# Placing each query tile's causal mask matmuls directly behind its scores

## The chip, the cores and the metric

The kernel runs on one core of a Trainium2 chip. The metric is the device time of one launch in microseconds (us). Lower is better. The engines are called by their names in the profile: PE is the tensor engine's matmul stream and PEld its weight loads, DVE the vector engine, ACT the scalar engine, POOL the GpSimd engine, SP the engine that issues most of the DMAs.

## The reference

The reference is a two-layer decoder block over 8 batches of 256 tokens of 512 features: cross-attention to an image context, a quantised feed-forward layer, a second cross-attention, and a last block with latent causal self-attention and a mixture of experts. Only the causal self-attention of that last block is touched. Cut to what matters, for each batch and each of 16 heads (`HD` = 32):

```python
scores = jnp.einsum('bqhd,bkhd->bhqk', q, k) * scale
causal = jnp.tril(jnp.ones((s, s), dtype=bool))
scores = jnp.where(causal[None, None], scores, jnp.finfo(scores.dtype).min)
probs = jax.nn.softmax(scores, axis=-1)
out = jnp.einsum('bhqk,bkhd->bqhd', probs, v).reshape(b, s, H)
```

## The kernel before, in words

The program is written as five stages, one behind the other, each with its own instruction stream per engine. Nothing schedules them: the order on an engine is the order in which the Python code issues the instructions, and semaphores join the engines. The stage in question is `latent_attention`. It works through the 8 batches in nine turns of `for i in TURNS` (i = -1 to 7). In turn i, PE finishes the attention of batch i and prepares batch i+1, and the two are woven together.

The 16 heads of a batch are taken in four calls (c = 0 to 3) of four heads (j = 0 to 3). A head has 32 features, so its query and key lie on 32 partitions, and the four heads of a call lie on the four partition groups of 32. `scores(s, c)` computes the scores of batch s for the sole purpose of finding each query's peak. For each of the two query tiles (t = 0 and 1, of 128 queries) it issues three products of split operands (`qt_hi` by `kt_lo`, `qt_hi` by `kt_hi`, `qt_lo` by `kt_hi`), each for four heads. Each of these matmuls uses 32 rows of the array, and the four heads of a product use four different row groups. This text calls four such matmuls a tiled group. Query tile t writes columns t·128 to t·128+255 of four banks of `s_ps`, one bank for each head.

The causal mask is added on PE too: a full-array matmul of the bf16 identity `ident_b` with the bf16 matrix `mask` (-1e30 above the diagonal) accumulates onto the 128x128 diagonal block of a head. There are eight of these in a call: four heads for each of two query tiles. The last of them raises `s_ready`. `find_peak` on DVE waits for it, reduces the two query tiles with two instructions (L2714 and L2715) and raises `peak_done`, and only then may the next call of `scores` start, for it overwrites `s_ps`.

There are 32 calls of `scores` in the stage: four in turn -1 for batch 0, and four in each of the turns 0 to 6. In those turns PE has other work between the calls: `inverses` and `outputs` (the projection with `first_out` and `wq`), `values`, and from the next turn on `latents` and `turn_peaks`. `turned_scores` (L2408 and L2411) computes the scores a second time, transposed, with the same kind of tiled groups, and `weigh` and `masses` (L2425 and L2436) use tiles of 32 columns. In the trace, `L47`, `L48` and `L49` are the three products of the helper `split_product`, all with full-array matmuls, and L2318 is a full-array transpose.

Of the kernel before, what the change touches and what calls it, by code (L numbers as in the profile page):

```python
# [25 lines left out]
TB = SEQ // P  # L26
# [2064 lines left out]
def latent_attention(nc, x_res, h_res, h_sq, ident, begun, handed, picks, w_dram, rope_dram, late, expert_dram, expert_rows):  # L2091
# [24 lines left out]
    with ExitStack() as ctx:  # L2116
# [82 lines left out]
        def await_free(eng, name, s):  # L2199
            eng.wait_ge(free_of(name, s), use_of[name, s] // BANKS + 1)  # L2200
# [106 lines left out]
        def _(pe):  # L2307
# [66 lines left out]
            def scores(s, c):  # L2374

                if c == 0:
                    if s > 0:
                        pe.wait_ge(exp_done, 2 * C * s)
                    for name in ("kt0", "kt1", "qt0", "qt1"):
                        await_free(pe, name, s)  # L2380
                else:
                    pe.wait_ge(peak_done, C * s + c)
                for t in range(TB):
                    tok = slice(t * P, (t + 1) * P)
                    cols = slice(t * P, t * P + SEQ)
                    for n, (q, k) in enumerate(((qt_hi, kt_lo), (qt_hi, kt_hi), (qt_lo, kt_hi))):
                        for j in range(4):
                            mine = slice(HD * j, HD * (j + 1))
                            pe.matmul(s_ps[:, j, cols], q[mine, c, tok], k[mine, c, :], start=n == 0, stop=n == 2)
                for t in range(TB):  # L2390
                    for j in range(4):
                        mm = pe.matmul(s_ps[:, j, 2 * t * P:(2 * t + 1) * P], ident_b[:, :], mask[:, :], start=False, stop=True,
                                       skip_group_check=True)
                mm.then_inc(s_ready, 1)
# [64 lines left out]
            for i in TURNS:  # L2459
# [41 lines left out]
                if nxt:  # L2501
                    if i == -1:
                        pe.wait_ge(mask_done, 1)
                    scores(i + 1, 0)
# [9 lines left out]
                if nxt:  # L2514
                    scores(i + 1, 1)
                if now:
                    outputs(i, 1, 0)
                if nxt:
                    values(i + 1, 1)
                    scores(i + 1, 2)  # L2520
# [1054 lines left out]
```

## Time and profile before

| What | us |
|---|---|
| Median of 3 runs | 2353.2 |
| Lowest and highest run | 2352.92, 2355.69 |
| The profiled execution | 2352.92 |
| Its span in the trace | 2351.2 |
| PE busy in the span | 2200.7 (94%) |
| DVE, ACT, POOL busy | 1317.1, 999.1, 798.4 |

The busy shares are means over all stages. The calls of `scores` start between 1717.8 and 1995.4 us of the span; what they are worth has to be read from that stretch. In a row of the timeline, several instructions of one line that follow each other are merged; the row gives the start of the first, the time to the end of the last, and the count. A matmul's duration contains its way through the array, so consecutive matmuls overlap, and the distance between their starts is what each costs PE.

### The profile page before, as it was taken

Reading aid. Unit: us, or ns where it says so; the run is one execution under the profiler, and the core shown is the slowest. Engines: PE = TensorE matmul, PEld = TensorE weight load, DVE = VectorE, ACT = ScalarE, POOL = GpSimd, SP = SyncE. Lnnn points to the kernel's source line nnn. Section 1 sums busy time; section 2 is a strip of 40 time slices with the busy share of each in tenths; the row PEclk is TensorE's granted clock in tenths of the full one; section 3 lists DMA queues with packets and bytes.
Section 4 is the critical chain, followed back from the end, with each engine's and each line's share of the span. In section 5 each row is a group of like instructions: output and inputs, shape, how many; then the busy total and the mean of one; then the engine's idle time right before and its main releaser. Section 6 shows DMA issues by size and latency. Waiting matters only on the chain. (4 is left out here: it accounts for less than half of the span.)

```text
span 2351.2 us, 42185 instructions
## 1 busy us (share of the span) xinstructions
PE 2200.7 (94%) x17406; PEld 1806.1 (77%) x17406; DVE 1317.1 (56%) x2355; ACT 999.1 (42%) x1770; POOL 798.4 (34%) x687
## 2 busy tenths in 40 slices
PE   6999998689979999999999999999889999899996
PEld 4666676344458888898999998988768787799996
DVE  6666775588874344433443335444554545677764
ACT  4777433377843223222332223222255554425553
POOL 3111110366522222222323222333154553224664
PEclk9999998799989999999999999999999999899998
DMA  6454202100021002111111012110000000247996
GB/s 251 159 170 131 73 2 109 54 1 1 1 81 66 34 28 81 72 37 37 46 54 69 31 36 97 37 46 19 1 25 2 2 2 28 82 152 238 274 274 120
DMA packets 45342, 177.49 MB, mean 75 GB/s; under 512 B 5984, under 2 KB 5984, under 8 KB 38880
## 3 DMA queue, kind: packets, MB, share of 16 engines
q1 hardware_dynamic: 35296, 151.72, 18.2%
q0 software_dynamic: 9856, 23.07, 4.8%
q8 instruction: 139, 2.28, 0.4%
q14 instruction: 51, 0.42, 0.1%
HBM read 143.84 MB, written 30.93 MB: 74 GB/s over the span
## 5 line engine op out<-in xcount | busy, mean ns | idle before, releaser
L247 POOL TENSOR_TENSOR c_prob<-c_prob,c_inv_mass 128x512 f32<-128x512 f32 x128 | 130.4, 1040 | 438.0 <-DVE c_inv_mass L239 438.0
L229 ACT ACTIVATE c_prob<-c_s_ps,c_neg_peak 128x256 f32<-128x256 f32 x256 | 117.8, 473 | 360.6 <-DVE c_neg_peak L218 360.6
L47 PE MATMUL c_ring<-bc_xt_lo,bc_wq_hi 128*128 128x256 f32 x512 | 152.1, 297 | 5.4 <-POOL bc_xt_lo L1675 5.4
L47 PE MATMUL c_ring<-c_ctx_lo,c_w_hi 128*128 128x256 f32 x512 | 146.5, 286 | 0.0
L48 PE MATMUL c_ring<-bc_xt_hi,bc_wq_hi 128*128 128x256 f32 x512 | 146.2, 286 | 0.0
L49 PE MATMUL c_ring<-bc_xt_hi,bc_wq_lo 128*128 128x256 f32 x512 | 146.1, 285 | 0.0
L49 PE MATMUL c_ring<-c_ctx_hi,c_w_lo 128*128 128x256 f32 x512 | 143.4, 280 | 0.0
L48 PE MATMUL c_ring<-c_ctx_hi,c_w_hi 128*128 128x256 f32 x512 | 143.2, 280 | 0.0
L1679 POOL TENSOR_TENSOR c_ctx_lo<-c_ctx_f,c_ctx_hi 128x1024 fp32r<-128x1024 f32 x32 | 78.2, 2444 | 166.9 <-ACT c_ctx_hi L1868 166.9
L203 PE MATMUL c_s_ps<-c_kt,c_qt 128*128 128x256 f32 x512 | 121.7, 381 | 3.0 <-ACT c_prob L229 3.0
L1201 POOL TENSOR_TENSOR b_hw<-b_h,b_lnw 128x512 f32<-128x512 f32 x64 | 96.2, 1519 | 78.8 <-DVE b_h L1375 78.8
L1675 POOL TENSOR_TENSOR bc_xt_lo<-c_xt_f,bc_xt_hi 128x1024 fp32r<-128x1024 f32 x32 | 79.1, 2471 | 127.4 <-ACT bc_xt_hi L1862 127.4
L286 PE MATMUL c_o_ps<-c_prob_t,c_v 128*128 128x256 f32 x512 | 117.6, 384 | 0.9 <-ACT c_prob_t L276 0.9
L2052 DVE SCALAR_TENSOR_TENSOR x_res<-c_ring,c_gain,x_res 128x512 f32<-128x512 f32 x64 | 47.8, 750 | 114.0 <-PE c_ring L49 114.0
L295 DVE TENSOR_TENSOR c_o_lo<-c_o_ps,c_o_hi 128x1024 fp32r<-128x1024 f32 x32 | 39.2, 1224 | 127.6 <-ACT c_o_hi L291 127.6
L47 PE MATMUL c_ring<-c_w_lo,c_ctx_hi 128*128 128x512 f32 x256 | 110.2, 430 | 0.0
L286 PEld LDWEIGHTS c_o_ps<-c_prob_t,c_v 128*128 128x128 f32 x512 | 98.2, 193 | 15.3 <-issue 1.3
L1944 DVE COPY c_kt<-c_ring 128x512 f32<-128x512 f32 x64 | 44.2, 691 | 116.7 <-PE c_ring L49 116.7
L1944 DVE COPY c_qt<-c_ring 128x512 f32<-128x512 f32 x64 | 44.3, 691 | 116.2 <-PE c_ring L49 116.2
L203 PEld LDWEIGHTS c_s_ps<-c_kt,c_qt 128*128 128x128 f32 x512 | 94.9, 190 | 16.4 <-ACT c_prob L229 3.8
L3023 POOL DMA_INDIRECT out<-el_r,e_target x44 | 81.4, 1849 | 72.7 <-DMA out<-el_r,e_target 57.9
L47 PEld LDWEIGHTS c_ring<-bc_xt_lo,bc_wq_hi 128*128 128x128 f32 x512 | 99.5, 194 | 6.6 <-POOL bc_xt_lo L1675 5.8
(540 smaller groups left out, 6980.5 us busy)
## 6 DMA issues: line engine op xcount, KB each, us to landing
x_res<-b_w SPq DMA_DIRECT2D x48, 512.0 KB, 4.7
e_raw<-e_w SPq DMA_DIRECT2D x15, 1536.0 KB, 8.7
bc_raw<-c_w SPq DMA_DIRECT2D x16, 1024.0 KB, 5.9
c_ctx_f<-ctx_t SPq DMA_DIRECT2D x32, 512.0 KB, 3.5
c_xt_f<-xnt_scratch SPq DMA_DIRECT2D x24, 512.0 KB, 3.2
h_res<-e_w SPq DMA_DIRECT2D x7, 1536.0 KB, 10.1
wq_scratch<-x_res SPq DMA_DIRECT2D x24, 256.0 KB, 2.5
ab_wq<-wq_scratch SPq DMA_DIRECT2D x3, 2048.0 KB, 13.1
```

The lines of the kernel that those rows point to most:

```text
L47: pe.matmul(out, lhs[0], rhs[1], start=first, stop=False)
L48: pe.matmul(out, lhs[0], rhs[0], start=False, stop=False)
L49: return pe.matmul(out, lhs[1], rhs[0], start=False, stop=last)
L203: mm = pe.matmul(self.s_ps[:, j, 0:w], q_of(u, j), k_of(u, j)[:, 0:w], start=mask is None, stop=True, skip_group_check=mask is not None)
L229: ins = act.activation(self.prob[:, u % 2, j, 0:w], self.s_ps[:, j, 0:w], ACT.Exp, bias=self.neg_peak[:, u % 2, j:j + 1], scale=self.scale ...
L247: pool.tensor_tensor(part, part, self.inv_mass[:, u % 2, js].unsqueeze(2).to_broadcast([P, 2, w]), ALU.mult).then_inc(self.prob_done, 1)
L286: mm = pe.matmul(out_of(g, j), v_of(g, j, t), self.prob_t[:, buf, t, j, :], start=(t == 0), stop=(t == TB - 1))
L1201: pool.tensor_tensor(hw[:, n % 2, cols], h[:, n % 2, cols], lnw[:, cols], ALU.mult).then_inc(hw_done, 1)
L1675: pool.tensor_tensor(xt_lo[:, :, :], xt_f[:, :, :], f32(xt_hi[:, :, :]), ALU.subtract).then_inc(xt_lo_done, 1)
L1679: pool.tensor_tensor(ctx_lo[:, :, :], ctx_f[:, :, :], f32(ctx_hi[:, :, :]), ALU.subtract).then_inc(ctx_lo_done, 1)
L1944: dve.tensor_copy(to, bank_of(f"f{k}", s)).then_inc(free_of(f"f{k}", s), 1)
L3023: pool.indirect_dma_start(out=out[:, :], out_offset=bass.IndirectOffsetOnAxis(ap=target[:, TB * j + t:TB * j + t + 1], axis=0), in_=r[:, j ...
```

## The change

One line is removed: the second `for t in range(TB):` loop. The four mask matmuls of a query tile now stand inside the first loop, behind the three tiled groups of the same query tile. Before, they stood in a loop of their own behind both query tiles. The matmuls, their operands, flags and counts are the same, and so is the semaphore, which the last mask matmul of the call raises.

```diff
--- before.py
+++ after.py
@@ -2387,7 +2387,6 @@
                         for j in range(4):
                             mine = slice(HD * j, HD * (j + 1))
                             pe.matmul(s_ps[:, j, cols], q[mine, c, tok], k[mine, c, :], start=n == 0, stop=n == 2)
-                for t in range(TB):
                     for j in range(4):
                         mm = pe.matmul(s_ps[:, j, 2 * t * P:(2 * t + 1) * P], ident_b[:, :], mask[:, :], start=False, stop=True,
                                        skip_group_check=True)
```

On PE, the end of call c = 0 of batch 0 changes as follows (the first turn; `d_kt`, `d_qt` are keys and queries, L2318 turns the inputs of batch 1):

```order
 L2389 MATMUL d_s_ps<-d_kt_hi,d_qt_hi 128x256 x4
 L2389 MATMUL d_s_ps<-d_kt_hi,d_qt_lo 128x256 x4
+L2391 MATMUL d_s_ps<-d_mask,d_ident_b 128x128 x4
 L2389 MATMUL d_s_ps<-d_kt_lo,d_qt_hi 128x256 x4
 L2389 MATMUL d_s_ps<-d_kt_hi,d_qt_hi 128x256 x4
 L2389 MATMUL d_s_ps<-d_kt_hi,d_qt_lo 128x256 x4
-L2392 MATMUL d_s_ps<-d_mask,d_ident_b 128x128 x8
+L2391 MATMUL d_s_ps<-d_mask,d_ident_b 128x128 x4
 L2318 MATMUL d_ring<-ident,d_a 128x128 x8
```

Four of the eight mask matmuls moved up: they now stand behind the third tiled group, and four stay behind the sixth. The line number drops by one, since the file is a line shorter.

On PE in a later turn, where `outputs` (here with `d_first_out`) follows a call of `scores`:

```order
 L2389 MATMUL d_s_ps<-d_kt_hi,d_qt_hi 128x256 x4
 L2389 MATMUL d_s_ps<-d_kt_hi,d_qt_lo 128x256 x4
+L2391 MATMUL d_s_ps<-d_mask,d_ident_b 128x128 x4
 L2389 MATMUL d_s_ps<-d_kt_lo,d_qt_hi 128x256 x4
 L2389 MATMUL d_s_ps<-d_kt_hi,d_qt_hi 128x256 x4
 L2389 MATMUL d_s_ps<-d_kt_hi,d_qt_lo 128x256 x4
-L2392 MATMUL d_s_ps<-d_mask,d_ident_b 128x128 x8
+L2391 MATMUL d_s_ps<-d_mask,d_ident_b 128x128 x4
 L47 MATMUL d_ring<-d_first_out_lo,d_o_hi 128x512
 L48 MATMUL d_ring<-d_first_out_hi,d_o_hi 128x512
```

The same four moved, and what follows the call is the same full-array product. No other engine's order changes.

## Rows read from the trace of the kernel before

**Rows 1.** Part 1 of the page: busy time, share of the span, instructions.

```profile
PE 2200.7 (94%) x17406; PEld 1806.1 (77%) x17406; DVE 1317.1 (56%) x2355; ACT 999.1 (42%) x1770; POOL 798.4 (34%) x687
```

**Rows 2.** Busy time in stretches: turns 0 to 6, and one turn of them.

```profile
core 0: us, PE busy (x) PEld busy (x) DVE busy (x) ACT busy (x) POOL busy (x), PEclk, DMA share, GB/s
1741.00:1983.00 242.00, 239.78 (x3348) 190.68 (x3346) 126.16 (x165) 128.89 (x221) 129.27 (x186) 1.00 0.02 5
1870.81:1908.09 37.28, 37.03 (x509) 29.53 (x508) 19.26 (x25) 19.87 (x35) 19.26 (x27) 1.00 0.01 2
```

**Rows 3.** All waits of PE between 1741 and 1983: total, times, longest.

```profile
PE d_ring L2318 <- DVE d_qt_lo L2707: 1.7, 7, 0.3
PE d_s_ps L2389 <- DVE d_kt_lo L2707: 0.5, 1, 0.5
```

**Rows 4.** Timeline of PE, a call of `scores`: start, us, instruction, count, idle before.

```profile
1874.26 0.40 PE L49 MATMUL d_ring<-d_first_out_hi,d_o_lo 128*128 128x512 f32 x1
1874.59 0.39 PE L2389 MATMUL d_s_ps<-d_kt_lo,d_qt_hi 32*128 32x256 f32 x4
1874.81 0.29 PE L2389 MATMUL d_s_ps<-d_kt_hi,d_qt_hi 32*128 32x256 f32 x4
1874.93 0.28 PE L2389 MATMUL d_s_ps<-d_kt_hi,d_qt_lo 32*128 32x256 f32 x4
1875.05 0.29 PE L2389 MATMUL d_s_ps<-d_kt_lo,d_qt_hi 32*128 32x256 f32 x4
1875.17 0.29 PE L2389 MATMUL d_s_ps<-d_kt_hi,d_qt_hi 32*128 32x256 f32 x4
1875.29 0.28 PE L2389 MATMUL d_s_ps<-d_kt_hi,d_qt_lo 32*128 32x256 f32 x4
1875.51 0.62 PE L2392 MATMUL d_s_ps<-d_mask,d_ident_b 128*128 128x128 bf16 x8
1875.94 0.47 PE L47 MATMUL d_ring<-d_first_out_lo,d_o_hi 128*128 128x512 f32 x1
```

**Rows 5.** Line 2392 of PE: count, shortest, median and longest duration in ns.

```profile
L2392 PE MATMUL d_s_ps<-d_mask,d_ident_b x256: 218/220/267, 1718.7 to 1995.4; 128*128 128x128 bf16 x128
```

**Rows 6.** Timeline of PE, full-array matmuls of 256 columns before a tiled group.

```profile
1891.29 0.28 PE L48 MATMUL d_ring<-bc_wq_hi,bc_xt_hi 128*128 128x256 f32 x1
1891.41 0.28 PE L49 MATMUL d_ring<-bc_wq_hi,bc_xt_lo 128*128 128x256 f32 x1
1891.62 0.39 PE L2408 MATMUL d_s_ps<-d_qt_hi,d_kt_lo 32*128 32x256 f32 x4
```

**Rows 7.** Timeline of PE, the last call for batch 0 and what follows.

```profile
1729.05 0.67 PE L2392 MATMUL d_s_ps<-d_mask,d_ident_b 128*128 128x128 bf16 x8
1733.36 0.58 PE L47 MATMUL d_ring<-bc_xt_lo,bc_latent 128*128 128x256 f32 x1 [3.64 <-POOL bc_xt_lo L2233]
```

**Rows 8.** Timeline of ACT in the first turn.

```profile
1719.80 1.09 ACT L2545 ACTIVATE d_at_f<-d_ring 128x512 f32<-128x512 f32 x2 [2.94 <-PE d_ring L2318]
1720.97 1.06 ACT L2551 ACTIVATE bc_xt_hi<-d_at_f 128x1024 fp32r<-128x1024 f32 x1
1721.93 2.91 ACT L2538 ACTIVATE h_res<-x_res,bc_shift,bc_row_rstd 128x512 f32<-128x512 f32 x4
1724.75 0.57 ACT L2577 ACTIVATE d_v<-d_ring 128x512 f32<-128x512 f32 x1
1725.23 1.04 ACT L2531 ACTIVATE d_first_out_hi<-d_raw 128x1024 fp32r<-128x1024 f32 x1
```

**Rows 9.** Timeline, behind the last call for batch 7.

```profile
1994.97 0.62 PE L2392 MATMUL d_s_ps<-d_mask,d_ident_b 128*128 128x128 bf16 x8
1995.63 0.69 DVE L2714 TENSOR_REDUCE d_neg_peak<-d_s_ps 128x4 f32<-128x512 f32 x1 [0.78 <-PE d_s_ps L2392]
1997.51 0.44 PE L2371 MATMUL d_ring<-ident,d_neg_peak 128*128 128x128 f32 x2 [1.92 <-DVE d_neg_peak L2715]
```

**Rows 10.** Busy time in stretches around the end of the first turn.

```profile
1721.00:1729.50 8.50, 5.18 (x99) 4.13 (x99) 3.83 (x5) 6.22 (x8) 3.15 (x2) 1.00 0.01 3
1729.50:1736.30 6.80, 3.16 (x17) 2.94 (x14) 1.82 (x2) 0.00 (x0) 3.81 (x2) 0.50 0.00 0
```

## The prediction, made before the changed kernel ran

> **What bounds the kernel now.** I read the page's busy times first, then the stretches, then PE's waits, then the timeline of one call. PE is busy 94% of the span [rows 1], but that is a mean over five stages. In the 242 us between 1741 and 1983, which hold the calls of `scores` of turns 0 to 6, PE is busy 239.78 us at a granted clock of 1.00, while DVE, ACT and POOL are busy about half of the time [rows 2]. PE's waits of that stretch sum to 2.2 us: seven short ones for the split of the turned queries and one for that of the turned keys [rows 3]. None of them stands behind a wait for a peak: the four calls of a turn are far enough apart that DVE's reduction is done. So in turns 0 to 6, what PE spends more or less goes straight into the time. A turn takes 37.28 us with 37.03 us of PE [rows 2]. The chain of waits begins only after this stage, so it says nothing of it; the stretches do.
>
> **What the call costs.** The timeline of one undisturbed call shows four distances [rows 4]. Tiled groups follow each other at 0.12 us (1874.93, 1875.05, 1875.17, 1875.29). The first mask matmul starts 0.22 us after the sixth group: 0.10 us late. The eight masks end 0.62 us after the first began and one lasts 0.22 us [rows 5], so they follow each other at (0.62 - 0.22) / 7 = 0.057 us. At the call's begin, the step from full-array to tiled work shows two losses. The first tiled group starts only when the full-array matmul before it has 0.07 us left of its duration: 1874.26 + 0.40 - 0.07 = 1874.59 [rows 4]. The same is seen behind a shorter one: 1891.41 + 0.28 - 0.07 = 1891.62, where without a switch the distance was 0.12 us [rows 6]. And the first tiled group lasts 0.39 us instead of 0.28 and the second starts 0.22 us after it instead of 0.12: its weights are not loaded ahead.
>
> **The change, term by term.** It removes nothing and adds no instruction. It moves four mask matmuls per call from the end to the middle, and there PE has to switch from tiled to full-array and back once more.
>
> - Into the masks, behind the third group: 0.22 instead of 0.12 us, +0.10.
> - The four masks themselves: 4 x 0.057 us in the middle, 4 x 0.057 us fewer at the end, 0.
> - Back to the tiled groups, behind the fourth mask: this step without a wait isn't in the trace of before. By the rule of the two rows above, the group starts 0.07 us before the mask's end: 0.22 - 0.07 = 0.15 us after its start instead of 0.057, +0.09. From below it is bounded by the masks' own distance (+0.00), from above by the longest distance seen into a tiled group, 0.33 us behind a 512-column matmul [rows 4], +0.27. I take 0.09, since the 256- and the 512-column row obey one rule although they differ in distance.
> - The first tiled group of the second query tile loads its weights uncovered: 0.22 instead of 0.12 us between starts, 0.39 instead of 0.28 in duration, +0.11. Bounded below by 0 (weights hidden under the masks).
> - The end of the call, from the last tiled group to mask and from mask to the next work, is as it was: 0.
>
> The sum is 0.10 + 0.09 + 0.11 = 0.30 us per call, with bounds of 0.10 and 0.48.
>
> **How many calls are on the path.** There are 32. The 28 of turns 0 to 6 are, by the above, since PE doesn't idle there. The last call for batch 7 is among them: DVE waits for its masks (0.78 us), PE waits for DVE (1.92 us), and a later mask shifts the rest [rows 9]. Of the four calls of the first turn, three are hidden: behind the last one PE idles 3.64 us until POOL has split the inputs of batch 1 [rows 7], and three later calls take 3 x 0.30 = 0.9 us of this. If that cover were gone they would cost these 0.9 us. The first of the four is not hidden: behind it stand the transposes of batch 1's inputs, for which ACT waits (2.94 us), and from then on ACT works without a gap through 1726.3 [rows 8] toward the very split that PE waits for. So 28 + 1 = 29 calls count: 29 x 0.30 = 8.7 us.
>
> On the other engines nothing moves. What hangs on `s_ready` is `find_peak`, now 0.30 us later behind each call; in turns 0 to 6 the next call comes later by the same, so no new wait forms.
>
> The profiled execution took 2352.92 us, 1.7 us more than its span and 0.3 us less than the median. Its sum is 2352.92 + 8.7 = 2361.6; from the median it is 2353.2 + 8.7 = 2361.9 us, +0.37%.
>
> **A rule weighed.** In the rows, the successor of another shape starts 0.07 us before the recorded end of the matmul before it, at each of the three switches [rows 4, 6]. The Trainium skill, TensorEngine Tiling (Array Packing), Key Properties, says that a change of the tiling mode drains the engine. Taken word for word, with nothing begun before the end, each of the two added switches would cost 0.07 us more, 0.44 us per call in all. The trace agrees with the rule in kind and shows the drain overlapped by these 0.07 us.
>
> The other rule speaks for a smaller price. Within tiled work the trace shows weights loaded ahead, since the groups stand 0.12 us apart; at a switch it does not, by the 0.39 us group [rows 4]. The Trainium skill, TensorE: Matmul & The Clock Gate, The mechanism, says that a weight load is pulled ahead of matmuls in flight when its row group doesn't conflict or the background buffer takes it. The masks fill all row groups, so the background buffer would have to take it; what that gives is the second rival.
>
> **The rivals.**
>
> 1. *Full drain.* Each added switch waits for the complete end of the matmuls before it: (0.30 + 2 x 0.07) x 29 = 12.8 us, 2366.0 us. For it: only that the step from a mask to a tiled group hasn't been seen undisturbed. Against it: the 0.07 us hold for both directions.
> 2. *Weights hidden, only the entry counts.* The second tile's weights are loaded under the masks, and the step out of the masks costs no more than their own distance: 0.10 x 29 = 2.9 us, 2356.1 us, within 0.2%. For it: there are four masks of 0.057 us, time enough for a load. Against it: in rows 4 and 6 the load ahead would have had a longer matmul to hide under, and didn't.
> 3. *The delay doesn't reach the end.* Another engine's chain sets the pace of a turn, and PE's 0.30 us fall into its idle time: about 2353.2 us. Against it: 0.25 us of idle PE in a turn of 37.28 [rows 2] can't take in 4 x 0.30 us, and even these waits follow PE's own transposes.
> 4. *The other side: the masks ride in the shadow of the tiled groups.* A tiled group lasts 0.28 us but costs 0.12; the remaining 0.16 us are its way through the array. If masks that stand between two query tiles could run in that shadow, four of them, 4 x 0.057 = 0.23 us, would vanish from each call: 29 x 0.23 = 6.7 us less, 2346.5 us. It decides from an added price below zero, so only if the mask follows a group at 0.12 us or sooner. Against it: the same step at the call's end takes 0.22 us [rows 4].
>
> The clock moves the sum a little: after the first turn's calls it falls to 0.50 from 1729.5 to 1736.3, where PE had waited for DVE and then for POOL [rows 7, 10]. PE's idle time there shrinks from 3.64 to 2.7 us. If the clock stayed up, the work from 1733.36 to 1736.3 would take half: at most 1.5 us back. This stays inside the range of the forecast.
>
> **How the numbers follow.** A change of 0.2%, 4.7 us, is about what a measurement of this kernel can tell from none. The forecast has 0.80, the full drain 0.07, hidden weights 0.06, a delay that doesn't arrive 0.04, the shadow 0.03. The forecast's own range comes from the roundings of the rows, 0.27 to 0.34 us per call, from 29 to 32 calls, from the clock, and from a median that may stand an us off: 0.27 x 29 - 1.5 - 1 = 5.3 up to 0.34 x 32 + 1 = 11.9 us, 2358.5 to 2365.1. I let the range reach to the full drain at the upper end, 2366.2, and leave out the others, 0.13 in sum. Slower has 0.80 + 0.07 = 0.87; within 0.2% 0.06 + 0.04 = 0.10; faster 0.03.
>
> **What would show it.** In the changed kernel's timeline, a call should read: third tiled group, +0.22 us the first mask, four masks at 0.057, +0.15 us behind the fourth a tiled group of 0.39 us, +0.22 us the next. A turn should take 37.28 + 4 x 0.30 = 38.5 us with PE's idle time unchanged, and the wait for POOL behind the first turn should be shorter by 0.9 us. A turn of 37.7 us would speak for hidden weights, one of 39.0 for a full drain, one of 37.3 for a delay absorbed elsewhere. The prediction is wrong if masks follow a tiled group at 0.12 us, or if PE's idle time in turns 0 to 6 falls.

## The result, and the profile after

| | before | after |
|---|---|---|
| Median of 6 runs, us | 2354.44 | 2369.61 |
| Lowest and highest, us | 2351.43, 2358.65 | 2364.32, 2374.07 |
| Span of the trace, us | 2351.2 | 2364.0 |

The ratio of after to before is 1.0057 (95% interval 1.0043 to 1.0073), 13.4 us slower. It rests on 19 executions of the changed kernel, whose median is 2367.82 us; the table has the first six of them. Measured twice more against new runs of before, the ratio was 1.0055 (1.0037 to 1.0073) and 1.0042 (1.0028 to 1.0056). The direction was forecast; the time lies above the range of 2358.5 to 2366.2, and even the range's upper end is 3.4 us short of it.

The page of after, part 1, answers to [rows 1]. The instructions are the same, and PE is busy 14.6 us longer, more than the time between the spans.

```profile
PE 2215.3 (94%) x17406; PEld 1809.9 (77%) x17406; DVE 1316.0 (56%) x2355; ACT 1000.6 (42%) x1770; POOL 794.9 (34%) x687
```

The timeline of PE in after, a call at the same place of a turn (turn 0), answers to [rows 4]:

```profile
1767.62 0.40 PE L49 MATMUL d_ring<-d_first_out_hi,d_o_lo 128*128 128x512 f32 x1
1767.94 0.39 PE L2389 MATMUL d_s_ps<-d_kt_lo,d_qt_hi 32*128 32x256 f32 x4
1768.17 0.29 PE L2389 MATMUL d_s_ps<-d_kt_hi,d_qt_hi 32*128 32x256 f32 x4
1768.29 0.28 PE L2389 MATMUL d_s_ps<-d_kt_hi,d_qt_lo 32*128 32x256 f32 x4
1768.50 0.40 PE L2391 MATMUL d_s_ps<-d_mask,d_ident_b 128*128 128x128 bf16 x4
1768.83 0.39 PE L2389 MATMUL d_s_ps<-d_kt_lo,d_qt_hi 32*128 32x256 f32 x4
1769.05 0.28 PE L2389 MATMUL d_s_ps<-d_kt_hi,d_qt_hi 32*128 32x256 f32 x4
1769.17 0.28 PE L2389 MATMUL d_s_ps<-d_kt_hi,d_qt_lo 32*128 32x256 f32 x4
1769.39 0.40 PE L2391 MATMUL d_s_ps<-d_mask,d_ident_b 128*128 128x128 bf16 x4
1769.59 0.47 PE L47 MATMUL d_ring<-d_first_out_lo,d_o_hi 128*128 128x512 f32 x1
```

Every step is as forecast. The first mask starts 0.21 us after the third group. The fourth mask starts 0.18 us after the first (0.40 - 0.22), and the next tiled group 0.15 us after that: 1768.83. That group lasts 0.39 us, and its successor starts 0.22 us later. From the first tiled group to the first product behind the call, after takes 1.65 us; before took 1.35 us [rows 4].

The stretch of turns 0 to 6 and one turn of it in after, against [rows 2]; then the waits of PE from 1741 to 1995, against [rows 3]:

```profile
1741.00:1983.00 242.00, 240.50 (x3187) 187.92 (x3190) 122.93 (x163) 123.91 (x213) 122.88 (x175) 1.00 0.01 2
1763.89:1802.44 38.55, 38.30 (x513) 29.76 (x512) 17.91 (x23) 19.94 (x35) 19.28 (x27) 1.00 0.01 2
```

```profile
PE d_ring L2318 <- DVE d_qt_lo L2706: 1.8, 7, 0.3
PE d_s_ps L2389 <- DVE d_kt_lo L2706: 0.5, 1, 0.5
```

A turn takes 38.55 us instead of 37.28, and PE is idle for the same 0.25 us in it. No wait is new.

What was not forecast is the first turn. Here are three stretches of before, each cut at the start of the first tiled group of a call: the first turn (first call for batch 0 to first call for batch 1), the 24 calls for batches 1 to 6, and from the last call of all to the first matmul of the expert stage. The columns are those of [rows 2]; the third from the right is the granted clock.

```profile
1717.79:1758.95 41.16, 33.15 (x488) 26.66 (x488) 24.52 (x40) 21.40 (x35) 22.58 (x28) 0.92 0.01 2
1758.95:1982.18 223.23, 221.27 (x3041) 176.37 (x3041) 112.40 (x141) 117.49 (x202) 115.21 (x162) 1.00 0.01 4
1994.05:2027.30 33.25, 22.75 (x324) 16.40 (x323) 17.63 (x27) 14.01 (x23) 9.52 (x11) 0.88 0.01 1
```

And the same of after, with two parts of its first turn behind them:

```profile
1720.48:1763.85 43.37, 37.83 (x488) 29.82 (x488) 24.32 (x40) 21.55 (x35) 22.59 (x28) 0.84 0.01 2
1763.85:1994.68 230.83, 228.79 (x3041) 177.78 (x3041) 112.47 (x141) 117.76 (x202) 115.25 (x162) 1.00 0.01 4
2007.30:2042.48 35.18, 24.59 (x323) 17.92 (x323) 17.63 (x27) 14.03 (x23) 9.63 (x11) 0.85 0.00 1
...
1721.90:1725.30 3.40, 3.19 (x28) 2.63 (x24) 1.82 (x2) 1.53 (x3) 0.00 (x0) 0.50 0.00 0
1732.10:1742.30 10.20, 7.96 (x55) 7.05 (x56) 2.42 (x4) 0.39 (x1) 5.22 (x3) 0.50 0.01 2
```

The 24 calls grew by 7.60 us, 0.32 each, at a clock of 1.00. The first turn grew by 2.21 us, not by 0.3: the clock fell to 0.50 (1.2 GHz) twice, for 3.4 and for 10.2 us, where it had fallen once in before, for 6.8 us [rows 10]. The last stretch grew by 1.93 us, 1.6 us more than its one call explains.

The same stretches in all traces (us; the last column is from the first matmul of `latent_attention` to the last of the expert stage):

| Kernel | First turn | 24 calls | Last call to expert stage | Both stages |
|---|---|---|---|---|
| before | 41.16 | 223.23 | 33.25 | 629.2 |
| before, again | 41.14 | 223.17 | 33.23 | 629.2 |
| after | 43.37 | 230.83 | 35.18 | 639.9 |
| after, second | 43.36 | 230.81 | 35.09 | 639.8 |
| after, third | 43.38 | 230.74 | 33.70 | 639.5 |
| first batch only | 43.33 | 223.30 | 33.38 | 628.2 |
| later batches only | 41.28 | 230.79 | 34.84 | 637.4 |
| one mask in the middle | 43.49 | 230.83 | 33.67 | 639.6 |
| after, filled | 41.63 | 230.74 | 34.58 | 638.6 |
| first call only | 43.36 | 223.25 | 34.74 | 632.2 |
| first call delayed | 42.87 | 223.24 | 34.51 | 630.4 |
| same delay, no switch | 43.22 | 230.66 | 36.01 | 640.5 |
| no masks | 41.06 | 214.39 | 32.68 | 617.1 |
| no masks, filled | 40.95 | 214.27 | 32.68 | 617.9 |

One stretch isn't in the table, from the stage's first matmul to the first call of `scores`. It takes 12.80 to 12.83 us in twelve of the fourteen traces. In two variants, the first batch alone and the same delay in all calls, it takes 11.28 and 11.45 us, and the clock doesn't fall in it, although nothing ahead of the first call differs. Here it is for before, the first batch alone and the same delay:

```profile
1704.97:1717.79 12.82, 9.57 (x55) 8.30 (x56) 6.25 (x15) 6.34 (x11) 4.96 (x9) 0.87 0.34 106
...
1707.55:1718.83 11.28, 8.26 (x55) 6.93 (x56) 7.06 (x15) 6.34 (x11) 5.24 (x9) 1.00 0.39 121
...
1708.10:1719.55 11.45, 8.25 (x55) 6.95 (x56) 7.22 (x15) 6.34 (x11) 5.25 (x9) 1.00 0.38 119
```

So in these two the falls of the clock lay differently from the start, and their first turns can't be set beside the others alone.

### The profile page after: what moved, and what is told of

Read it like the earlier page. It is cut to its first block and busy times, and to the rows that moved or that the text cites. A ratio compares the mean times of both kernels' runs of the same rounds, so it can differ in the third digit from the quotient of the medians.

```text
span 2364.0 us, 42185 instructions
## 1 busy us (share of the span) xinstructions
PE 2215.3 (94%) x17406; PEld 1809.9 (77%) x17406; DVE 1316.0 (56%) x2355; ACT 1000.6 (42%) x1770; POOL 794.9 (34%) x687
```

## The experiments

All of them change `scores` alone, except the filled ones and the three that repeat a kernel. The ratio is always to the kernel before, run on the same chip. The diffs are against the kernel before and are cut: `pe.matmul(...)` stands for the mask matmul as it was. Two variants, the first call alone and the first call delayed, were executed once each, so only their traces are read.

**The changed kernel again.** 

> The changed kernel once more, to see what repeats. In its first trace each call of scores in turns 0 to 6 costs 0.31 us more, 28 of them 8.7 us, as forecast. But the first turn cost 2.2 us where 0.3 was forecast (clock at 0.50 for 13.7 us instead of 6.8), and 2.7 us were lost before the stage began. Theory A (clock): the extra switches make PE's clock fall for longer in the first turn, in every execution; then the first turn again costs 1.5 to 2.5 us more than 0.3, and the time is 11 to 13 us over before. Theory B (chance): the extra is where clock dips happen to fall; then the first turn costs 0.3 to 1 us in this trace, and the time over many runs is 9 us over before.

Measured: ratio 1.0055 (1.0037 to 1.0073); first turn 43.36 us at clock 0.84, as in the first trace. The first turn's extra repeats, and so does its absence in the second trace of before (41.14 us): it belongs to the kernel. A part of the first trace's difference was chance all the same: the stage begins at 1705.0 us in the trace of before and at 1707.7 and 1710.4 in these two, with no instruction changed ahead of it.

**The first batch alone.** 

> Only the four calls of scores for batch 0 (the first turn) have their masks placed per query tile; the 28 others are as before. Theory A (the first turn's clock falls longer because of the switches): 2 to 3 us slower than before, with more than 6.8 us at clock 0.50 between the first call and turn 0. Theory B (chance): 0.3 us slower, no difference that can be measured, and the calls of turns 0 to 6 cost what they did.

```diff
-                for t in range(TB):
-                    for j in range(4):
+                    for tt, j in ([(t, j) for j in range(4)] if s == 0 else []):
                         mm = pe.matmul(...)
+                for tt, j in ([] if s == 0 else [(t, j) for t in range(TB) for j in range(4)]):
+                    mm = pe.matmul(...)
```

Measured: ratio 1.0001 (0.9990 to 1.0012). The trace has the longer first turn, with the clock mean that after has in it:

```profile
1718.83:1762.16 43.33, 37.41 (x489) 29.39 (x490) 24.53 (x40) 21.52 (x35) 22.58 (x28) 0.84 0.01 2
```

Both stages together are 1.0 us shorter than before. The first turn is 2.2 us longer, but the stretch ahead of the first call is 1.5 us shorter (11.28 instead of 12.82), and the expert stage ran 1.8 us faster. From the stage's first matmul to the first call for batch 1 the extra is thus only 0.6 us (54.61 against 53.98), so this trace doesn't show what the four calls cost. The time doesn't either: its interval goes from -2.4 to +2.8 us. The trace of the first call alone, below, has the usual 12.80 us ahead of it and decides.

**The later batches alone.** 

> The four calls of the first turn are as before, the 28 of turns 0 to 6 have their masks placed per query tile. Theory A: 28 x 0.31 = 8.7 us slower, the first turn as in the kernel before. Theory B: also 8.7 us, so this one and the changed kernel differ by 0.3 us. A third reading, that the extra comes behind the stage (the last turn and the start of the expert stage at another phase), gives 11 us or more here.

The edit is the same with the two conditions exchanged. Measured: ratio 1.0035 (1.0022 to 1.0048), 8.2 us with an interval of 5 to 11 us. The trace:

```profile
1720.55:1761.83 41.28, 33.21 (x489) 26.77 (x490) 24.52 (x40) 21.42 (x35) 22.60 (x28) 0.92 0.01 2
1761.83:1992.62 230.79, 228.76 (x3042) 177.81 (x3041) 112.47 (x141) 117.60 (x202) 115.28 (x162) 1.00 0.02 4
```

The first turn is as before, and the 24 calls have grown by 7.56 us. Both stages together are 8.2 us longer, near the forecast's 8.7. The interval can't tell this from the 10.7 us of the changed kernel's trace; the 41.28 us of the first turn in the trace can.

**One mask in the middle, seven at the end.** 

> One mask matmul instead of four stands between the two query tiles of every call; the other seven stand at the end. If the price is that of the two switches of shape (0.10 in, 0.09 out, 0.11 for the first tiled group) and not of the masks, a call of turns 0 to 6 again costs 0.31 us more, and a turn 38.5 us. If each mask in the middle has a price of its own, a quarter of it stays: 0.08 us a call, a turn of 37.6 us.

```diff
-                for t in range(TB):
-                    for j in range(4):
+                    for tt, j in ([(0, 0)] if t == 0 else []):
                         mm = pe.matmul(...)
+                for tt, j in [(t, j) for t in range(TB) for j in range(4)][1:]:
+                    mm = pe.matmul(...)
```

Measured: ratio 1.0051 (1.0036 to 1.0067), the 24 calls 230.83 us. The middle of a call in its trace:

```profile
1769.99 0.28 PE L2389 MATMUL d_s_ps<-d_kt_hi,d_qt_lo 32*128 32x256 f32 x4
1770.21 0.23 PE L2391 MATMUL d_s_ps<-d_mask,d_ident_b 128*128 128x128 bf16 x1
1770.37 0.39 PE L2389 MATMUL d_s_ps<-d_kt_lo,d_qt_hi 32*128 32x256 f32 x4
1770.59 0.29 PE L2389 MATMUL d_s_ps<-d_kt_hi,d_qt_hi 32*128 32x256 f32 x4
```

One mask costs the call as much as four did: 0.22 us in, 0.16 us out (0.23 - 0.07), and again a group of 0.39 us. The price is that of the two switches, and a mask in the middle adds none of its own.

**The kernel before as a control.** 

> The kernel before itself, as a control: what its trace shows when taken again. In the first trace of it, the stage of scores begins at 1705.0 us of the span; in the traces of five variants it begins 2.6 to 5.4 us later, although no instruction ahead of it differs. If that is chance, this trace begins later too (1707 to 1710), and the ratio to the kernel before is 1.000 within 0.15%. The first turn, from the first call of scores to the first call of turn 0, should again take 41.2 us if its length belongs to the kernel; if it varies by chance, up to 43.4 us as in the four variants with switches in the first turn.

Measured: ratio 0.9991 (0.9980 to 1.0003). The stage begins at 1707.0, 2.1 us later than in the first trace, and then repeats it to 0.06 us in every stretch up to the expert stage. So what lies ahead of the stage differs from run to run, and the stage's own length didn't in these two.

**PE kept at work in the first turn.** 

> The changed kernel with 118 added mask-sized bf16 matmuls (0.057 us each) into the unused output bank where PE waits in the first turn (15, 18, 30 and 55 of them, 0.9 to 3.1 us, shorter than the waits of 1.0, 1.2, 1.9 and 3.6 us). Theory A (PE's idle stretches and switches in the first turn let the clock fall, which costs 1.9 us over the forecast): with PE kept at work the clock stays up, the first turn shrinks from 43.4 to about 40 us, and the time falls by 3 us against the changed kernel, to a ratio of about 1.004. Theory B (the clock falls by chance, or the idle time is not what matters): first turn 43 us, ratio 1.0055.

```diff
+            def filler(count):
+                for _ in range(count):
+                    pe.matmul(o_ps[:, 0, 0:P], ident_b[:, :], mask[:, :], start=True, stop=True)
```

Measured: ratio 1.0034 (1.0024 to 1.0044); the first turn takes 41.63 us. The calls of `filler` are added where the expectation says, in the first turn alone. The clock of that turn, first the low stretch and then the rest:

```profile
1722.00:1725.40 3.40, 3.40 (x29) 3.34 (x27) 1.82 (x2) 1.67 (x3) 0.00 (x0) 0.50 0.00 0
1725.40:1762.10 36.70, 36.06 (x555) 29.35 (x553) 21.55 (x36) 19.82 (x33) 22.62 (x28) 1.00 0.01 2
```

The short fall of 3.4 us stays, the long one of 10.2 us is gone, and the turn is 1.74 us shorter although PE has 118 matmuls more to do. It is gained behind the wait for POOL: PE takes that work up 17.37 us after the first call's start (16.89 in after: the last fill runs on past the end of POOL's split, which comes at 1737.3 in this trace), and from there to the first call for batch 1 it needs 24.26 us instead of 26.48. So the low clock is what most of the first turn's extra was lost to. The forecast of 40 us had both falls gone.

**The first call alone.** 

> Only the very first call of scores (batch 0, c = 0) has its masks placed per query tile. In the four variants whose first turn has the switches, a clock dip begins 1 to 2 us behind the first call's start, and the later one lasts 10.2 instead of 6.8 us. If the first call's switches bring the first of these dips, the trace shows it here, and the first turn takes 42 us or more. If it needs the switches of all four calls, the trace reads as before: one dip of 6.8 us, 41.5 us (0.3 more for this call).

The edit is that of the first batch alone, with the condition `s == 0 and c == 0`.

Measured: the first turn takes 43.36 us at clock 0.84, behind the usual 12.80 us. The two falls of 3.4 and 10.2 us are those of after. The switches of one call, 0.3 us, bring the whole 2.2.

**The first call delayed, without a switch.** 

> The order of before; behind the first call's masks (batch 0, c = 0) six mask matmuls once more, 0.34 us, no switch. With the switches in this one call the first turn took 43.37 us. If the switches did it, 41.5 us here; if a third of a microsecond's delay is enough, 43.4 us.

```diff
-                for t in range(TB):
-                    for j in range(4):
+                for tt, j in [(t, j) for t in range(TB) for j in range(4)] + (
+                        [(1, j) for j in range(4)] + [(1, 3)] * 2 if s == 0 and c == 0 else []):
                         mm = pe.matmul(...)
```

Measured: 42.87 us, 1.71 more than before for an added 0.34. Here are the first turn, the low stretch in it, and PE's first work behind the wait:

```profile
1721.36:1764.23 42.87, 35.16 (x494) 28.64 (x494) 24.52 (x40) 21.52 (x35) 22.32 (x28) 0.88 0.01 2
...
1733.10:1743.30 10.20, 6.87 (x35) 6.61 (x34) 2.33 (x4) 0.84 (x3) 4.12 (x2) 0.50 0.00 0
```

```profile
1737.28 0.58 PE L47 MATMUL d_ring<-bc_xt_lo,bc_latent 128*128 128x256 f32 x1 [3.33 <-POOL bc_xt_lo L2233]
```

In before, PE came back from the wait at 1733.36 [rows 7] and had worked 2.9 us when the clock rose at 1736.3. Here it came back at 1737.28, 4.2 us into the low stretch instead of 3.9, and the clock rose only at 1743.3, after 6 us of work at half speed. No switch was added, so the long stretch needs none: in this trace a third of a microsecond's delay was enough. It is different with the short fall of 3.4 us. It isn't here, while each of the seven traces with switches in the first call has a fall that begins 0.9 to 1.8 us after that call's start. Of the seven traces without them only the next variant's has one there. That the switches bring this fall is likely from this, but not shown.

**The same delay in all calls, without a switch.** 

> The order of before, and at the end of each of the 32 calls of scores five or six mask matmuls once more (5.5 x 0.057 = 0.31 us, added to elements that are masked already). So each call is as much longer as in the changed kernel, but with full-array work instead of two switches of shape. Turns 0 to 6 should again grow by 28 x 0.31 = 8.7 us under every theory. If the switches make the clock fall in the first turn, the first turn here has one dip of 6.8 us and takes 41.5 us, as before plus 0.3. If it is the delay or its phase that does it, 43.4 us. The last turn (30.0 us before, 31.6 to 31.9 in kernels that arrive there 8 to 11 us later) takes 31.6 or more if that is a matter of when it starts, 30.3 if it is the switches. In time: ratio 1.0037 or so in the first case, 1.0050 in the second.

```diff
-                for t in range(TB):
-                    for j in range(4):
+                for tt, j in [(t, j) for t in range(TB) for j in range(4)] + (
+                        [(1, j) for j in range(4)] + [(1, 3)] * (1 + (c % 2 == 0))):
                         mm = pe.matmul(...)
```

Measured: ratio 1.0041 (1.0026 to 1.0057); first turn 43.22 us, the 24 calls 230.66 us. Its first turn and its last stretch:

```profile
1719.55:1762.77 43.22, 36.11 (x511) 29.55 (x511) 24.36 (x40) 21.52 (x35) 22.58 (x28) 0.92 0.01 2
...
2006.06:2042.07 36.01, 25.60 (x328) 18.86 (x328) 17.62 (x27) 14.02 (x23) 9.62 (x11) 0.81 0.01 2
```

Calls that are as long as in the changed kernel, with full-array work in place of the switches, give a kernel as slow as it, within the intervals. For the 24 calls this is what PE's work adds up to. The first turn agrees in length, but not in the way to it. Its mean clock is 0.92, with two falls of 3.4 us, and the first of them begins 0.6 us after the first call's start, ahead of the first added matmul. Here are the last three tiled groups of that call, which stand ahead of all its masks; the third takes 0.48 us where it took 0.31 in before:

```profile
1719.98 0.31 PE L2389 MATMUL d_s_ps<-d_kt_lo,d_qt_hi 32*128 32x256 f32 x4
1720.10 0.40 PE L2389 MATMUL d_s_ps<-d_kt_hi,d_qt_hi 32*128 32x256 f32 x4
1720.23 0.48 PE L2389 MATMUL d_s_ps<-d_kt_hi,d_qt_lo 32*128 32x256 f32 x4
```

So the delay can't have brought that fall. With the shorter stretch ahead of the first call, this run takes 54.67 us from the stage's first matmul to the first call for batch 1, against 53.98 in before and 56.19 in after. It doesn't show that a delay costs the first turn what the switches do.

**No mask matmuls.** 

> The eight mask matmuls of each call of scores are left out, so the peaks are found over all keys and not over the causal ones; a softmax doesn't depend on which peak is subtracted, and the causal cut of the probabilities by POOL stays. In the trace of before, the sixth tiled group to the second full-array product behind the masks takes 0.21 + 0.43 + 0.31 = 0.95 us; without masks it is 0.21 + 0.34 = 0.55 as behind L2411. So 0.40 us less per call, 29 calls on the path: 11.6 us faster than before, ratio 0.995. If a switch between two shapes cost nothing by itself, the gain would be the masks alone, 8 x 0.057 = 0.45 us a call and 13.1 us; if the calls weren't on the path, nothing.

```diff
-                            pe.matmul(s_ps[:, j, cols], q[mine, c, tok], k[mine, c, :], start=n == 0, stop=n == 2)
-                for t in range(TB):
-                    for j in range(4):
-                        mm = pe.matmul(...)
+                            mm = pe.matmul(s_ps[:, j, cols], q[mine, c, tok], k[mine, c, :], start=n == 0, stop=n == 2)
```

Measured: ratio 0.9952 (0.9937 to 0.9966), 11.3 us faster than before. The 24 calls take 214.39 us, 0.37 less each. A call of it in the timeline, from the sixth group on:

```profile
1765.32 0.29 PE L2389 MATMUL d_s_ps<-d_kt_hi,d_qt_lo 32*128 32x256 f32 x4
1765.54 0.50 PE L47 MATMUL d_ring<-d_first_out_lo,d_o_hi 128*128 128x512 f32 x1
1765.88 0.39 PE L48 MATMUL d_ring<-d_first_out_hi,d_o_hi 128*128 128x512 f32 x1
```

From the sixth group to the first product are 0.22 us; before they were 0.65 [rows 4]. Of these 0.43, 0.03 are lost to the product itself, which stands directly behind tiled work and takes 0.50 instead of 0.47. The switch stays, for full-array work must follow, and only the masks' own time goes. This version beats both kernels. Its first turn, 41.06 us, has a low stretch of 10.2 us too, from 8.6 us after the first call's start, with no delay added anywhere. It ends as early as in before (18.8 instead of 18.5 us), so its length alone doesn't make a turn longer. What counts is how much of PE's work behind the wait for POOL falls into it: 2.9 us in before, 3.7 here, 4.9 in after and 6.0 with the first call delayed.

**No masks, filled.** 

> The kernel without mask matmuls (the peaks over all keys), with the same 118 added matmuls where PE waits in the first turn. In the changed kernel they took the first turn from 43.4 to 41.6 us. Without masks the first turn takes 41.1 us with a clock dip of 10.2 us; PE waits there 0.9, 1.0, 1.9 and 4.8 us. If the fill keeps the clock up as there, the first turn takes 39 to 39.5 us and the time falls by a further 1.7 us, to a ratio of 0.9945 to before; if the fill only moves the waits, 0.9952 as without it.

Measured: ratio 0.9961 (0.9947 to 0.9974), no gain over the version without fill. The last fill ends at 1734.7, PE's wait for POOL only at 1737.04, and from there the clock is low for 3.4 us:

```profile
1732.00:1737.00 5.00, 2.75 (x50) 2.57 (x47) 1.44 (x2) 0.00 (x0) 4.99 (x3) 1.00 0.00 0
1737.00:1740.40 3.40, 3.36 (x15) 3.36 (x16) 0.00 (x0) 0.38 (x1) 0.00 (x0) 0.50 0.00 0
```

The expected gain of 1.7 us didn't come.

**A third measurement of the change.** 

> The changed kernel a third time, to see whether its timed excess is larger than what its traces add up. From the stage's begin to the last matmul of the expert stage, its two traces are 10.7 us longer than the two of before (639.8 and 639.9 against 629.1 and 629.2), a ratio of 1.0045; the two timed ratios were 1.0057 and 1.0055. If the trace has everything, the third ratio lies near 1.0045, the stretch again takes 639.8 us and the first turn 43.4 us. If the switches cost more in executions that aren't profiled, it lies at 1.0055 or above again.

Measured: ratio 1.0042 (1.0028 to 1.0056), first turn 43.38 us, both stages 639.5 us. The ratio lies near what the trace adds up to (10.3 us, 1.0044).

## Why the prediction was right or wrong

*PE bounds the stage:* right for turns 0 to 6. The 24 calls' 7.60 us arrived in full, and PE's idle time in a turn stayed at 0.25 us. *The delay doesn't reach the end* is out.

*The price of a call, 0.30 us:* right, and term by term. Measured 0.32 over the 24 calls; the rows of after show 0.21 us in, 0.15 out and the group of 0.39 us. The one unseen term, the step from a short mask back to a tiled group, was taken from the rule of two other rows (0.07 us before the end) and came out at 0.15 as worked out. In one of those two rows, at the begin of a call, PE's code also waits for `peak_done` at the same place, so the late load of the weights might have been that wait's. In the middle of a call no wait stands in the code, and the group takes 0.39 us there too: it is the change of shape. *Full drain* asked for 0.22 us there and *hidden weights* for a group of 0.28: both are out. The full drain's 2366.0 us came nearer to the measured time than the forecast did, for a reason that has nothing to do with it. *The masks in the shadow* is out by the 0.21 us. The experiment with one mask shows that the switches make the price.

*Three of the first turn's calls are hidden, and the fourth costs 0.30 us:* this step failed. The first turn cost 2.2 us. The order of the waits is as the prediction has it: PE still waits there for POOL's split. But that wait is 1.6 us shorter in the trace of after (2.01 instead of 3.64), not 0.9:

```profile
1737.37 0.58 PE L47 MATMUL d_ring<-bc_xt_lo,bc_latent 128*128 128x256 f32 x1 [2.01 <-POOL bc_xt_lo L2233]
```

What the prediction took for granted is that the clock's low stretch stays where it was or shrinks: "at most 1.5 us back", and nothing for a longer one. The runs showed a cost of 1.9 us in its place, at two points. First, a fall of 3.4 us came at the end of the first call, on the very path that the prediction calls not hidden. These are the transposes of batch 1's inputs, before and after:

```profile
1719.16 1.04 PE L2318 MATMUL d_ring<-ident,d_a 128*128 128x128 f32 x8
...
1722.33 1.91 PE L2318 MATMUL d_ring<-ident,d_a 128*128 128x128 f32 x8
```

They take 0.87 us longer, ACT and POOL follow them, and PE comes back from its wait 16.89 us after the first call's start instead of 15.57: 1.32 us later, where 0.30 was forecast. Second, the long low stretch lasted 10.2 us instead of 6.8, so 4.9 us of PE's work behind the wait ran at 1.2 GHz instead of 2.9 us: another 0.89 us. The two make the 2.21 us. With PE kept at work 1.74 us came back. A delay of 0.3 us in the first call alone, with switches or without, brought 2.2 and 1.7 us, in one trace each.

*The last call for batch 7 costs one more 0.30:* the stretch from it to the expert stage grew by 1.93, 1.85 and 0.45 us in the three traces of after. The expert stage behind it took 306.9 us in both traces of before and 305.1, 305.1 and 306.2 in those of after. The two changes sum to +0.1, +0.1 and -0.2 us, so the forecast's 0.30 for this call isn't seen in the sum, and no other cost is either. The clock's falls lie differently around the border of the two stages in before and after; that this hides the 0.30 isn't shown.

The sum of the trace is then 2.21 (first turn) + 7.60 (24 calls) + 0.75 (the next three) + 1.93 (last call and last turn) - 1.79 (expert stage) = 10.7 us, where 8.7 were forecast. That is a ratio of 1.0045. It lies within all three intervals. The mean of the three ratios, 1.0051, is 1.4 us above it; whether this difference is real isn't shown.

*The base and the range:* this failed too, beside the mechanism. The median of three runs, 2353.2, was below those that came later (2354.4, and 2354.2 to 2357.9 on the later occasions), and I allowed it 1 us. What lies ahead of the stage moved its begin between 1705.0 and 1710.4 us in 14 traces with the same instructions. Of the 7.7 us between forecast and measured median, 1.2 are the base and 2.0 are what the trace of after has over the 8.7. Another 1.8 go away with the median over all 19 executions (2367.82). The other 2.7 aren't assigned to a place: that the time fell so far above the range is only in part explained by the first turn.

## What to carry to other kernels

Keep matmuls of one array shape together: each change from four 32-row tiles to the full array and back cost 0.3 us here, for one matmul in between as for four, and it goes straight into a stage that PE bounds. Before moving full-array work into a tiled sequence, ask whether it is needed at all: a softmax may subtract the peak over all keys if the masked ones are cut later, and deleting the masks was worth more here than either place for them. This holds as long as no masked score lies so far above the others of its query that their exponentials vanish; no run here tries that. And where a stretch has PE waiting and the clock falling, don't book a shift of a few tenths as hidden: let the range reach up as well as down for the clock, by what the work costs at the low clock.

## What the runs showed of the hardware

- At a change of tile shape the next matmul starts 0.07 us before the recorded end of the last one, in both directions and for matmuls of 128, 256 and 512 columns (the profile models these ends). The first tiled group behind it isn't covered by an early weight load (0.39 instead of 0.28 us), even with four masks ahead of it.
- With 0.34 us of added PE work ahead of a wait, the clock's low stretch was 10.2 instead of 6.8 us and the turn 1.7 us longer, in one trace. What decides when the clock falls and rises was not tried.
- Traces of one kernel repeat a stretch of 223 or 231 us to 0.1 us, while the timed runs of before or of after, six or more together, spread over 7 to 14 us. In the traces the scatter lies ahead of the stage (its begin at 1705.0 to 1710.4 us) and behind the last matmul of the expert stage (16.4 to 21.3 us from there to the end).
